# Graph propagation for recommendation: GpSimd makes one of the two digit conversions of each message

## The reference

```
for _ in range(3):
    x = segment_sum(vals[:, None] * x[cols], rows, num_segments=18750)
    acc = acc + x
light = acc / 4                         # the same for the small embedding
users_emb = all_users[users] + upsample(mm_users[users])
items_emb = all_items + upsample(mm_items)
return sigmoid(users_emb @ items_emb.T + bias_user[users] + bias_item.T)
```

## Time and profile before

| | us |
|---|---|
| median of 3 runs | 7006.35 |
| lowest and highest | 6999.16, 7008.19 |
| span of the profiled execution | 7404.3 |
| DVE busy in it | 6190.8 |
| PE busy | 4555.1 |
| ACT busy | 4518.3 |
| POOL busy | 2314.9 |

### The profile page before, as it was taken

How to read it: one execution, slowest core, us unless ns; L and a number is a source line. 1 busy time by engine, 2 the same in 40 slices (tenths; PEclk the granted TensorE clock), 3 DMA queues, 4 the chain that set the end, 5 groups by cost and what they waited for, 6 DMA issues and landing times.

```text
span 7404.3 us, 186636 instructions
## 1 busy us (share of the span) xinstructions
PE 4555.1 (62%) x58016; PEld 3947.8 (53%) x58020; DVE 6190.8 (84%) x15385; ACT 4518.3 (61%) x10708; POOL 2314.9 (31%) x2100
## 2 busy tenths in 40 slices
PE   5300111037777777886666666788666666678879
PEld 4200111036666666885555555688555555568854
DVE  9999999988888888998777777899877777789970
ACT  0155444345555557997555555799655555579976
POOL 0144344024544441001555555100155555510000
PEclk9755555566766666665777777655577777755569
DMA  9400000025555555554444444455344444445536
GB/s 345 159 0 0 0 0 0 0 73 148 152 149 149 149 149 136 143 145 106 136 138 136 142 138 139 133 145 146 108 138 137 136 140 138 137 131 145 147 107 241
DMA packets 750539, 918.14 MB, mean 124 GB/s; under 512 B 71784, under 2 KB 607881, under 8 KB 750363
## 3 DMA queue, kind: packets, MB, share of 16 engines
q1 hardware_dynamic: 658540, 665.77, 33.3%
q0 software_dynamic: 91520, 250.84, 9.1%
q10 hardware_dynamic: 434, 1.05, 0.1%
HBM read 529.36 MB, written 388.09 MB: 124 GB/s over the span
## 4 chain that ended last, share of the span: by engine, by line
DVE 41%; issue 18%; DMA 11%; ACT 11%; PE 8%; another core or an unknown queue 5%; DVEq 3%; POOL 2%; SPq 1%; ACTq 0%; POOLq 0%
DVE ring L1172 12%; DMA ring<-posts 10%; DVE ring L1205 9%; ACT ring L633 5%; DVE ring L1201 4%; ACT ring L631 3%; PE psum L1457 3%; DVE store L990 3%; DVE store L988 2%; DVE total L820 2%; DVE store L998 2%; PE psum L1459 2%; DVE store L999 2%; POOL ring L714 2%
## 5 line engine op out<-in xcount | busy, mean ns | idle before, releaser
L621 ACT ACTIVATE ring<-ring 128x64 f32<-128x64 f32 x7584 | 2032.7, 340 | 1672.2 <-DVE ring L1172 1370.1
L1457 PE MATMUL psum<-ring 128*128 128x128 bf16 x15168 | 2259.1, 265 | 876.7 <-issue 411.8
L1457 PEld LDWEIGHTS psum<-ring 128*128 128x128 bf16 x15168 | 1838.0, 126 | 1159.0 <-issue 685.9
L743 POOL DMA_INDIRECT posts<-ring x1896 | 1851.5, 977 | 1826.8 <-ACT ring L621 1201.0
L1459 PE MATMUL psum<-ring 128*128 128x64 bf16 x15168 | 2189.9, 232 | 319.3 <-issue 313.5
L1459 PEld LDWEIGHTS psum<-ring 128*128 128x128 bf16 x15168 | 1708.8, 117 | 381.5 <-issue 378.9
L1172 DVE TENSOR_REDUCE ring<-psum 128x128 f32<-128x256 f32 x3792 | 1418.7, 416 | 6.6 <-remote 5.7
L1205 DVE TENSOR_SCALAR ring<-ring,lane_f 128x512 bf16<-128x512 bf16 x3792 | 1167.2, 350 | 0.0
L1201 DVE COPY ring<-store 128x384 bf16 x1896 | 510.7, 269 | 669.4 <-remote 531.4
L1494 PE MATMUL psum<-ring 128*128 128x64 bf16 x15168 | 1002.8, 244 | 0.0
L1494 PEld LDWEIGHTS psum<-ring 128*128 128x128 bf16 x15168 | 965.3, 167 | 0.0
(11 more groups left out here) (241 smaller groups left out, 4701.1 us busy)
## 6 DMA issues: line engine op xcount, KB each, us to landing
ring<-posts SPq DMA_DIRECT2D x474, 516.0 KB, 3.9
ring<-lanes_d SPq DMA_DIRECT2D x474, 512.0 KB
out<-ring SPq DMA_DIRECT2D x200, 250.0 KB, 2.0
posts<-store SPq DMA_DIRECT2D x2, 20640.0 KB, 115.8
posts<-store SPq DMA_DIRECT2D x2, 20124.0 KB, 88.6
posts<-ring POOLq DMA_INDIRECT x1896
ring<-runs_d SPq DMA_DIRECT2D x158, 128.0 KB
user_rows<-total SPq DMA_DIRECT2D x1, 1568.0 KB, 5.9
```

Of the source, the lines that this page charges most:

```text
L621: last = nc.scalar.activation(of, of, ACT.Copy, scale=vring[:, h, c * BLOCK + b:c * BLOCK + b + 1])
L743: pool.indirect_dma_start(out=posts[:, :], out_offset=bass.IndirectOffsetOnAxis(ap=dring[:, h, c:c + 1], axis=0), in_=msg[:, n, :], in_off ...
L1457: pe.matmul(psum[:, c, b * 2 * F:(b + 1) * 2 * F], of, parts[:, 0:2 * F], start=(k == 0), stop=False, skip_group_check=True)
```

## The change

Of the two digit conversions ACT keeps the first. POOL makes the second with a multiplication by a constant, in a loop of its own behind the scatters. It has a semaphore of its own, `s_seconds`, for which SP's next load and DVE's product wait as well. So that POOL doesn't overwrite digits that DVE still reads, it waits for `s_lows` of the message two before; `s_lows` and `s_seconds` are preset by 2 for that, and PE's wait for `s_lows` counts two more.

```diff
 (SP)
                         sp.wait_ge(s_digits, i * 2 + (layer * ITERS + s + 1))
+                        sp.wait_ge(s_seconds, i * 2 + (layer * ITERS + s + 1))
 (ACT)
-                        for k, scale in enumerate((2.0 ** -15, 2.0 ** -23)):
-                            last = nc.scalar.activation(digits[s][:, k, :].rearrange("p (u w) -> p u w", u=IU), got_byte[s][k],
-                                                        ACT.Copy, scale=scale)
-                        last.then_inc(s_digits, 1)
+                        nc.scalar.activation(digits[s][:, 0, :].rearrange("p (u w) -> p u w", u=IU), got_byte[s][0],
+                                             ACT.Copy, scale=2.0 ** -15).then_inc(s_digits, 1)
 (POOL)
+                pool.wait_ge(s_marked, layer + 1)
+                with pool.Fori(0, ITERS // 2) as i:
+                    for s in range(2):
+                        it = layer * ITERS + s
+                        pool.wait_ge(s_got[s], i * 16 + (layer * ITERS // 2 + 1) * 16)
+                        pool.wait_ge(s_lows, i * 2 + (it + 1))
+                        pool.sem_inc(s_pace, 1)
+                        nc.gpsimd.tensor_scalar(digits[s][:, 1, :].rearrange("p (u w) -> p u w", u=IU), got_byte[s][1],
+                                                2.0 ** -23, None, ALU.mult).then_inc(s_seconds, 1)
 (DVE)
+            dve.sem_inc(s_lows, 2)
+            dve.sem_inc(s_seconds, 2)
                     dve.wait_ge(s_digits, i * 2 + (it + 3))
+                    dve.wait_ge(s_seconds, i * 2 + (it + 3))
 (PE)
-                        pe.wait_ge(s_lows, i * 2 + (it + 1))
+                        pe.wait_ge(s_lows, i * 2 + (it + 3))
```

More of the change, by code:

```diff
@@ L325, in build @@
         s_digits = sem("s_digits")
+        s_seconds = sem("s_seconds")
         s_power = sem("s_power")
```

## The result

The changed kernel takes 7161.8 us (7157.61 to 7177.55, 4 runs), the kernel before 7006.76 beside it: ratio 1.0225, interval 1.021 to 1.0239, some 155 us more. The forecast was 7286, with a range of 7080 to 7620. The direction and the size class held; the way there, as the profile shows, was in good part another.

A forecast was written before the change was run, and what follows sets the result against it. The loop of load and ACT was taken to bound the second half at 3.67 us per message; DVE with POOL's hold would take 4.26, +0.59 x 474 = 280 us, so 7006 + 280 = 7286 us, range 7080 to 7620.

The forecast's parts named there:

- My sum: DVE per message: 3.46 + 1.2 - 0.4 = 4.26 us in place of 3.67, +0.59; over 474 messages 280 us.
- What bounds the kernel: Second half: the loop of load and ACT's conversions, 7.4 us over two buffers, allows one message in 3.7 us.
- the slow profiled execution (7404 us): The 280 us, made against the trace's 7404.3 us, were carried whole to the runs' median of 7006.35 us.
- (7.37 - 0.45) / 2 = 3.46 us: DVE's own work per message in the second half: two messages in 7.37 us, less 0.45 of waits for ACT.
- very best: Most to be had if DVE becomes the bound: 3.67 - 3.46 = 0.21 us per message, 100 us, 1.4%.
- I take 1.2 us: POOL's assumed time per second-digit conversion, between a memset and a two-input subtraction; bounds 0.95 and 2.37 us.
- third rival: POOL's conversion is as slow as its two-input subtraction or slower, from 1.89 us: 7566 us, at 2.37 us 7793; chance 0.10.
- They take turns, whole instructions at a time: DVE and POOL exclude each other on SBUF ports; 2.86 of DVE's 3.46 us per message exclude POOL.
- Hides 0.4 of its 1.2 us: POOL starts about 0.2 us into DVE's sum L1264, which hides 0.4 us; 0.8 stands before L1247 or L1250.
- The loop stops being the bound unless POOL is very late: Load, semaphores and the longer of ACT or POOL: even with 3.0 us for POOL, 3.6 us per message.
- fourth rival: The load's loop stays the bound, POOL finishing 3.5 us after landing: 3.85 us per message, 7090 us; chance 0.05.
- the signs that I had named: Profile after: loads 4.1 to 4.5 us apart, ACT waiting over 1 us, DVE operations lengthened except L1264, POOL 1.2 us plus waiting.

The follow-up runs named there:

- run 2: The changed kernel with all its waits, but POOL converts only 8 of the 1024 columns: 6854.3 us, ratio 0.9733.
- run 3: The changed kernel with four load buffers in place of two: 7128.1 us, ratio 1.0124.
- run 5: The kernel before with four load buffers and no conversion on POOL: 6973.6 us, ratio 0.9906.
- run 1: The kernel before plus a tail timing POOL's operations alone and beside DVE's; 7122 us with the tail, once; POOL's multiplication 2.77 us alone.
- run 6: The changed kernel, but POOL writes zeros over the second digits by memset and reads nothing: 6845.3 us, ratio 0.9726.
- 7: The changed kernel, but POOL casts the bytes with a plain copy, without the factor 2^-23: 7231.5 us, ratio 1.0272.
- 9: The changed kernel with POOL's plain cast, which waits for the lows of the message just before: 7360.9 against 7288.4 us on another chip, ratio 1.0107.
- run 4: The changed kernel with two load buffers, POOL converting four of the second digit's eight units and ACT the others: 6940.9 us, ratio 0.986.
- run 8: The changed kernel with four load buffers, POOL converting three of the second digit's eight units and ACT five: 6896.8 us, ratio 0.9793.

## Why the prediction was right, and where it wasn't

The account by measured parts, per message: 3.68 before; minus 0.41 for ACT's relief (run 2, 3.27); plus 0.58 for the hold that DVE can't hide (run 3, 3.85); plus 0.16 for two buffers, that is for the loop of load and POOL and, late in the third layer, for the worse start of the hold (4.01). Times 474: -194, +275, +76, together +157 us, against 155 measured. My sum had +0.59, and 280 us.

**What bounds the kernel: right in the main.** The loop of load and ACT was the limit: run 5 took it away and gained 68 us. That the slow profiled execution (7404 us) could stand for the others in this stage was right as well: 3.67 us there, 3.68 in run 1.

**"(7.37 - 0.45) / 2 = 3.46 us" for DVE: wrong, 3.27.** I took off only the idle times that the timeline prints in brackets. The starts show more: in the earlier trace rows L1247 and the next L1250 are 0.33 us apart, but L1250 (3117.60) and the next L1255 (3119.00) 1.40, where run 2 has 1.21. Over the pair it adds up to 7.37 - 2 x 3.27 = 0.83 us of waiting, not 0.45. So a "very best" of 100 us was 190. For PE I added durations that overlap: 3.38, where the chain gives 3.27.

**"I take 1.2 us" for POOL: wrong, 2.77,** above even the upper bound, 2.37. The middle between a memset and a two-input subtraction wasn't a price of a third kind of operation: a multiplication with one input is slower here than a subtraction with two. The Trainium skill's "roughly line-rate" for one input (GPSIMD Engine Reference, Engine selection), an estimate of 0.85 us, fits the cast's 1.04 and not this multiplication. By its length this was my third rival (0.10, "as slow as its two-input subtraction or slower"). Its condition came true and its price of 7566 us and more didn't, since it let POOL hold DVE for the whole length.

**"They take turns, whole instructions at a time": right in kind, too wide.** That DVE would be held up is the core of the forecast, and it is shown: runs 2 and 6 against 3, 7 and 9. The hold is 0.84 to 0.85 us for the two-input operations, as it seems the reading of 1024 elements, and not the operation's 2.77. L999 in the earlier trace rows couldn't tell these apart, since it is held for nearly the whole subtraction. That this is the time in which POOL reads its two tensors is likely, but not shown.

**"Hides 0.4 of its 1.2 us": less.** POOL started 0.27 us into the sum in run 3 and 0.43 in the message of the third layer above, not 0.2, and with two buffers often outside the sum. What the sum hid was 0.84 - 0.58 = 0.26 and 0.84 - 0.75 = 0.09 us.

**"The loop stops being the bound unless POOL is very late": wrong for two layers and a third of the last.** That was the fourth rival, to which I gave 0.05. Its 3.5 us for POOL was nearly what happened (3.69 with the wait for one DVE instruction); I had priced it at 7090 with 0.3 us for semaphores that are 0.58. It came about not by several DVE operations in turn but by POOL's own length.

So the errors in part cancelled. From the 280 us go 90 for DVE's floor (3.46 for 3.27) and 104 for the hold that isn't hidden (0.80 for 0.58); 76 come on top for the two buffers, for which the sum had no term, and 5 go for 3.68 in place of 3.67. A POOL operation taken as too short by 1.57 us and a hold taken as its whole length worked against each other in the second of these. That 7286 came within 125 us of the result is partly luck. Of the signs that I had named, ACT's waits (1.00 and 0.64 us for PE and the like), the unchanged sums and the lengthened DVE operations appeared; the spacing came out just under the 4.1 to 4.5, and POOL's own 2.77 us was the sign that I had named for the third rival.

## What to carry to other kernels

Before moving work to POOL, time that very operation: a cast and a multiplication over the same elements differ by 1.7 us here. Ask separately how long it runs, how long it reads, and what DVE does in that time, since the first sets chains of waits and the second DVE's loss. A small share, whose hold fits mostly beside an operation with an input in PSUM, was worth 1.4% here with two buffers (run 4), and 1.1% with four (6896.8 us in run 8 against 6973.6 in run 5), where the whole cost 2.2%. And take an engine's own work from starts in a stretch where nothing can wait, not from busy time less the idle that is printed.

## What the runs showed of the hardware that was not expected

- POOL's tensor-scalar takes 2.77 us for 1024 elements whatever the type or stride, and 1.49 for 512; its cast 1.04 us for 1024 (run 1).
- POOL's multiplication holds DVE's two-input products for 0.85 us of its 2.77; the 16-bit masks lose 1.7 us per conversion, in two holds (run 1). A memset of 0.95 us costs the products nothing (run 6), though one of 8.31 us held a copy for its whole length.
- PE's granted clock differed widely from run to run, and the time per matmul by under a tenth. Over the same 200 us (3100 to 3300), here for the kernel before taken again, the run with eight columns on POOL and the cast, it was 0.57, 0.92 and 0.50 (0.50 is its lower level, 1.2 GHz, throughout). PE took 176.61 us for 2633 matmuls, 193.62 for 2939 and 168.35 for 2338, that is 67, 66 and 72 ns each:

```profile
3100.00:3300.00 200.00, 176.61 (x2633) 169.55 (x2632) 186.51 (x275) 192.77 (x274) 0.00 (x0) 0.57 0.56 145
```

```profile
3100.00:3300.00 200.00, 193.62 (x2939) 189.55 (x2938) 200.00 (x306) 158.87 (x245) 63.63 (x62) 0.92 0.63 161
```

```profile
3100.00:3300.00 200.00, 168.35 (x2338) 154.92 (x2336) 200.00 (x244) 132.37 (x196) 56.61 (x49) 0.50 0.50 129
```
